# Attention and routed experts on one core: gathered tiles normalised by ScalarE, and no memsets between GpSimd's indirect transfers

## The reference

```
x = x + tanh(g_xattn) * attention(layernorm(x), ctx, ctx, Wq, bq, Wk, bk, Wv, bv)
n = layernorm(x)                         # (n - mean) / sqrt(var + 1e-5)
route = sigmoid(n @ Wr + br)             # 8 experts
e     = argmax(route);  p = max(route)
x = x + tanh(g_ffn) * p * (gelu(n @ W1[e]) @ W2[e])   # 128 -> 512 -> 128
```

## Time and profile before

| | |
|---|---|
| median of 3 runs | 146.72 us (146.46 to 148.03) |
| span of the profiled execution | 148.6 us |
| PE busy | 132.3 us, 89% |
| VectorE (DVE) busy | 96.4 us, 65% |
| ScalarE (ACT) busy | 77.9 us, 52% |
| GpSimd (POOL) busy | 121.3 us, 82% |
| DMA moved | 15.20 MB |

### The profile page before, as it was taken

How to read it: one execution, slowest core, us unless ns; L and a number is a source line. 1 busy time by engine, 2 the same in 40 slices (tenths; PEclk the granted TensorE clock), 3 DMA queues, 4 the chain that set the end, 5 groups by cost and what they waited for, 6 DMA issues and landing times.

```text
span 148.6 us, 4195 instructions
## 1 busy us (share of the span) xinstructions
PE 132.3 (89%) x1211; PEld 112.8 (76%) x1211; DVE 96.4 (65%) x532; ACT 77.9 (52%) x174; POOL 121.3 (82%) x198
## 2 busy tenths in 40 slices
PE   6989999989988976976899999999999999899690
PEld 2748777756755733854899899999999999899680
DVE  1698999997479999988659644455454345453230
ACT  0548597594584387328055274654555555454210
POOL 6538985887968988898998998998998998997354
PEclk9999999999999999999689999999999999999997
DMA  3999999911101151115413454551111100111000
GB/s 107 237 281 265 368 350 293 278 52 39 41 18 36 41 121 45 36 38 131 111 36 96 115 125 117 140 144 53 41 36 55 35 27 34 39 36 53 16 5 0
DMA packets 20080, 15.20 MB, mean 102 GB/s; under 512 B 6606, under 2 KB 16978, under 8 KB 20058
## 3 DMA queue, kind: packets, MB, share of 16 engines
q1 hardware_dynamic: 17328, 10.59, 27.2%
q0 software_dynamic: 2272, 4.27, 8.5%
q10 hardware_dynamic: 458, 0.08, 0.3%
HBM read 10.12 MB, written 5.26 MB: 103 GB/s over the span
## 4 chain that ended last, share of the span: by engine, by line
PE 53%; DVE 8%; issue 5%; POOL 1%; ACT 0%; DVEq 0%; POOLq 0%
PE banks_o L1309 24%; PE banks_v L1300 13%; PE bank_q L1300 5%; PE bank_p L1300 5%; PE bank_x L1292 3%; DVE rows L708 2%; PE bank_x L1172 1%; DVE stats L721 1%; POOL out_dram L448 1%; DVE tokn L926 1%; DVE rows L724 0%; DVE rows L775 0%; ACT hT L556 0%; DVE rank_max L742 0%; DVE tok L937 0%
## 5 line engine op out<-in xcount | busy, mean ns | idle before, releaser
L1309 PE MATMUL banks_o<-w_sb,hT 128*128 x312 | 42.6, 281 | 3.3 <-issue 1.8
L1309 PEld LDWEIGHTS banks_o<-w_sb,hT 128*128 128x128 f32 x312 | 38.5, 194 | 4.5 <-issue 4.4
L425 POOL DMA_INDIRECT scratch<-rows,row_at x32 | 31.8, 994 | 8.6 <-issue 4.5
L937 DVE SCALAR_TENSOR_TENSOR tok<-banks_o,tok 128x128 f32<-128x128 f32 x39 | 13.7, 350 | 35.3 <-PE banks_o L1309 22.5
L499 ACT COPY w_now<-w_sb 128x512 f32 x39 | 23.6, 611 | 10.3 <-issue 10.3
L442 POOL MEMSET unused<- 128x400 f32 x53 | 24.4, 461 | 0.0
L448 POOL DMA_INDIRECT out_dram<-tok x21 | 20.8, 991 | 3.5 <-issue 3.3
L448 POOL DMA_INDIRECT out_dram<-tok,token_at x18 | 17.7, 984 | 6.8 <-DVE tok L937 4.0
L1300 PE MATMUL banks_v<-toknT,w_now 128*128 128x128 f32 x160 | 22.0, 282 | 0.0
L556 ACT ACTIVATE hT<-banks_v 128x512 f32<-128x512 f32 x20 | 11.9, 596 | 17.5 <-PE banks_v L1300 10.7
L1300 PEld LDWEIGHTS banks_v<-toknT,w_now 128*128 128x128 f32 x160 | 20.3, 199 | 0.0
(11 more groups left out here) (176 smaller groups left out, 245.7 us busy)
## 6 DMA issues: line engine op xcount, KB each, us to landing
tok<-scratch SPq DMA_DIRECT2D x39, 66.0 KB, 2.2
x_all<-in_x_dram SPq DMA_DIRECT2D x8, 256.0 KB, 4.4
w_sb<-in_L_ffn_W_dram SPq DMA_DIRECT2D x1, 2048.0 KB, 10.5
ctx<-in_ctx_dram SPq DMA_DIRECT2D x8, 128.0 KB, 4.3
scratch<-pad_rows SPq DMA_DIRECT2D x1, 528.0 KB
scratch<-rows,row_at POOLq DMA_INDIRECT x32
out_dram<-tok POOLq DMA_INDIRECT x21
out_dram<-tok,token_at POOLq DMA_INDIRECT x18
```

The lines of the kernel that those rows point to most:

```text
L425: nc.gpsimd.indirect_dma_start(out=scratch, out_offset=bass.IndirectOffsetOnAxis(ap=row_at[:, g * GT + t:g * GT + t + 1], axis=0), in_=row ...
L937: nc.vector.scalar_tensor_tensor(out=tok[j][:, 0:D], in0=y_ps[j % 2], scalar=tok[j][:, SCALE:TOKEN], in1=tok[j][:, 0:D], op0=ALU.mult, op1 ...
L1309: last = nc.tensor.matmul(y_ps[j % 2], hT[j % DEEP][:, c * P:(c + 1) * P], w2_sb[:, bass.ds(w_at[j] + c * D, D)], start=(c == 0), stop=(c ...
```

## The change

The column of a row that held the mean now holds -mean * rstd, written by VectorE in a new instruction in `scale_logits`. `normalise_tile` moves from VectorE to ScalarE, as an Identity activation with that column as bias and rstd as scale. On ScalarE, `normalise_tile(0)` stands ahead of the first gelu, which loads the gelu table, `normalise_tile(1)` behind it, `normalise_tile(2)` behind the copies of W1 for tiles 2 and 3, and `normalise_tile(j + 3)` behind `gelu(j)` (and behind `tanh_logits` where there is one), ahead of `copy_w1(j + 4)`. `pause()` and its buffer and semaphore are gone, so that GpSimd's order keeps its transfers, its powers and its two normalisations alone.

```diff
-MEAN, RSTD, SCALE, TOKEN, ROW = 128, 129, 130, 131, 132
+SHIFT, RSTD, SCALE, TOKEN, ROW = 128, 129, 130, 131, 132
...
-            def pause():
-
-                if pauses[0]:
-                    pool.wait_ge(paused, pauses[0])
-                pauses[0] += 1
-                nc.gpsimd.memset(unused[:], 0.0).then_inc(paused, 1)
...
                 elif at in NORM_AT:
                     normalise_one(NG - 1, NORM_AT[at])
-                else:
-                    pause()
             for j in range(FFN_TILES):
                 scatter_tile(j)
-                if j < PAUSED:
-                    pause()
...
+            def normalise_tile(j):
+                if j < FFN_TILES:
+                    act.wait_ge(tok_in[j], 16)
+                    after(act, toknT_done, j - 2)
+                    nc.scalar.activation(tokn[j % 2][:], tok[j][:, 0:D], ACT.Identity, bias=tok[j][:, SHIFT:RSTD],
+                                         scale=tok[j][:, RSTD:SCALE]).then_inc(tokn_ready, 1)
...
+            normalise_tile(0)
             nc.scalar.activation(gelu_table[:], tanh_gates[:], ACT.Gelu)
+            normalise_tile(1)
             copy_w1(2)
             copy_w1(3)
+            normalise_tile(2)
             for j in range(FFN_TILES):
                 gelu(j)
                 if j == 1:
                     tanh_logits(NG - 2)
                 if j == 3:
                     tanh_logits(NG - 1)
+                normalise_tile(j + 3)
                 if j + DEEP < FFN_TILES:
                     copy_w1(j + DEEP)
...
                 nc.vector.tensor_tensor(scaled[:], rows[:, group(g), 0:E], column(g, RSTD).broadcast_to(wide), ALU.mult
                                         ).then_inc(scaled_done, 1)
+                nc.vector.scalar_tensor_tensor(out=column(g, SHIFT), in0=column(g, SHIFT), scalar=-1.0,
+                                               in1=column(g, RSTD), op0=ALU.mult, op1=ALU.mult)
...
-            def normalise_tile(j):
-                if j < FFN_TILES:
-                    dve.wait_ge(tok_in[j], 16)
-                    after(dve, toknT_done, j - 2)
-                    nc.vector.tensor_scalar(tokn[j % 2][:], tok[j][:, 0:D], tok[j][:, MEAN:RSTD], tok[j][:, RSTD:SCALE],
-                                            ALU.subtract, ALU.mult).then_inc(tokn_ready, 1)
```

More of the change, by code:

```diff
@@ L61, in attention_moe @@
     RSTD1_AT, NORM_AT = 2, {4: 0, 5: 1}
-    PAUSED = FFN_TILES - 8
     MOST = max(t1 - t0 for t0, t1 in STAGE_TILES)
@@ L149, in attention_moe @@
         place_of = sb("place_of", [P, GT, E])
-        unused = sb("unused", [P, 400])
         no_shift = sb("no_shift", [P, 1])
@@ L254, in attention_moe @@
         scattered = [sem(f"scattered{s}") for s in range(len(STAGES))]
-        paused = sem("paused")
         pads_ready, guards_written = sem("pads_ready"), sem("guards_written")
@@ L433, in _ @@
             normalise(6)
-            pauses = [0]
-            def pause():
-                if pauses[0]:
-                    pool.wait_ge(paused, pauses[0])
-                pauses[0] += 1
-                nc.gpsimd.memset(unused[:], 0.0).then_inc(paused, 1)
             def scatter_tile(j):
@@ L723, in bn_aggr2 @@
             def bn_aggr2(g, t):
-                return nc.vector.bn_aggr(rows[:, g * GT + t, E + MEAN:E + SCALE], stats2[:, t, :])
+                return nc.vector.bn_aggr(rows[:, g * GT + t, E + SHIFT:E + SCALE], stats2[:, t, :])
             def choose(c, step):
@@ L1069, in _ @@
                     take_tiles(0)
-            normalise_tile(0)
             sums(NG - 1)
@@ L1076, in _ @@
             residual(NG - 1, 1)
-            normalise_tile(1)
             choose(NG - 3, 0)
@@ L1084, in _ @@
             choose(NG - 3, 3)
-            normalise_tile(2)
             choose(NG - 3, 4)
@@ L1096, in _ @@
             aggregate2(NG - 1, 1)
-            normalise_tile(3)
             aggregate2(NG - 1, 2)
@@ L1108, in _ @@
             sum_tiles(1)
-            normalise_tile(4)
             pass_experts(1)
@@ L1122, in _ @@
                     choose(NG - 1, 1)
-                    normalise_tile(5)
                     choose(NG - 1, 2)
@@ L1127, in _ @@
                     copy_transposed(n + 1)
-                    if j > 0:
-                        normalise_tile(n + 2)
                 if j == 0:
```

## The result

The changed kernel took 143.67 us (median of 4 runs, 143.02 to 144.07) against 147.28 for the kernel before (4 runs, 146.46 to 148.03): a ratio of 0.974, 95% interval 0.969 to 0.979. That is faster, by 3.6 us where 2.9 were forecast. The same kernel was 9.5% slower on two chips it was run on later (ratios of 1.095 and 1.094), which no step of the prediction allows for. Both have to be explained.

The account below looks back on a forecast made before the run. PE bounds the stream of expert tiles, so only the start could gain: 3.0 us (1.6 clock, 1.3 order) less 0.1 for added VectorE work, memsets 0; 146.72 - 2.9 = 143.8 us, 8-in-10 range 143.0 to 146.8.

Parts of the forecast that it names:

- step 5: The start: with ScalarE normalising, PE transposes tile 5 at 68.05 instead of 69.81 and tile 7 3.0 us sooner.
- the bound of 70: Sign for the start: the prediction is wrong if `tanh(7)` on ScalarE lies beyond 70 us.
- the clock: Part of the start's gain: `down(2)` and `up(5)` on PE at 2.4 GHz instead of 1.2, 1.6 us.
- the order: Part of the start's gain: tile 5 no longer waits behind VectorE's routing of group 7, 1.3 us.
- rival B: ScalarE bounds the start, its queue behind tile 5's load making `tanh(7)` late: 148.1, up to 148.9 us; chance 0.10.
- steps 1 to 3: VectorE loses 39 `tokn`; ScalarE gains 39 at 515 ns, hidden in the stream; VectorE's eight added instructions cost 0.1 us.
- rival D: Identity under the gelu table forces ScalarE table loads, two per tile over 39 tiles: some 245 us; chance 0.02.
- step (4): GpSimd loses 53 memsets of 461 ns, 0.3 us won per transfer; counted as 0, bounds 0 and 0.4 us gained.
- 0.12 for slower: Chance given to the kernel being over 1% (1.47 us) slower.
- the prediction's own signs: It is wrong if `tanh(7)` lies beyond 70, the low clock remains, or the stream's beat exceeds 1.89 us.
- with nothing further recorded around it: Claim about the profiled execution before: span 148.6 us, 1.9 above the median of three runs (146.72).

Follow-up runs that it names:

- e8: The changed kernel with the 22 memsets among the scatters into scratch put back, none among the output transfers, on chip 3: 158.33 us, ratio 1.054.
- r2_before: The kernel before, without an edit, profiled again on chip 3: 149.42 us, ratio 0.998.
- e3: The kernel before with more filler matmuls on PE around the transpose of tile 5 (seven ahead, four behind), on chip 2: 152.09 us, ratio 1.005.
- r1_changed: The changed kernel, without an edit, run on chip 3: 164.41 us, ratio 1.095 to the kernel before.
- e1: The kernel before with only the memset pauses taken out, VectorE still normalising, on chip 2: 168.59 us, ratio 1.112.
- e2: The changed kernel with all 53 memsets put back, ScalarE normalising, on chip 2: 150.73 us, ratio 0.995 to the kernel before.
- e10: The changed kernel with all memsets, tile 5 normalised right behind tanh of group 7, PE's register reads ahead of its fillers, chip 4: 150.09 us, ratio 0.9925.
- e4: The changed kernel without the four filler matmuls ahead of the transpose of tile 5, on chip 2: 165.03 us, ratio 1.090 to the kernel before.

## Why the prediction was right, and where it failed

**Right: the start (step 5).** Transpose of tile 5 forecast at 68.05, measured 67.63; `down(2)` 69.5 and 68.76; `copy_transposed(5)` 70.2 and 69.59; `up(5)` 70.5 and 70.14; transpose of tile 7 73.0 and 72.42 on the chain; `tanh(7)` 69.0 and 68.18, well inside the bound of 70. Each is 0.4 to 0.8 us early, and so is the first load of stage 1 (issued at 64.63, forecast at 65.3). The 2.9 us from tile 0 to tile 7 stand between traces of two chips, but on chip 3 alone the transpose of tile 7 is 3.0 us earlier in e8 than in r2_before, which is the forecast (3.0, less 0.1). The split fits too: e3 gives the clock 1.5 us on PE (1.6 forecast), and from `down(1)` to `down(4)` PE needs 10.90 us in r2_before and 8.15 in e8, 2.75 less, which leaves 1.2 for the order (1.3 forecast). One number in rival B is off: by its own step of 1.5 us from the landing of tile 5 to `tanh(7)`, tile 5 at 68.7 gives 70.2 and not 69.8; nothing hangs on it.

**Right: the costs on ScalarE and VectorE (steps 1 to 3).** `tokn` takes 483 ns against 515 taken, within 411 to 615. There is no second table load, so rival D falls. ScalarE is busy 8.0 of 10 us in the stream (8.4 forecast), and the beat stays at 1.89. The added VectorE instructions take 0.15 us each (157 ns taken).

**Right as a number, wrong as a model: step (4).** The step was "I take 0 for the memsets, bounds 0 and 0.4 gained through less blocking of VectorE". The pitch of 1.28 us came as forecast (68.62, 69.89). On chip 1 nothing contradicts the price: no wait of the changed kernel was held there, and the 0.7 us by which 3.6 exceeds 2.9, above the upper bound of 0.4, is less than the four runs of before are apart. On three other chips the memsets are not free work to be taken away but what keeps the other engines' waits from being held: without them 1.112, 1.095 and 1.094, with them 0.995. The missing term is 5 to 8 us on the chain of waits for each of two rows of eight or more transfers (6.90 and 5.27 in r1_changed, 7.38 and 8.14 in e1), and the idle PE's low clock behind them. The prediction had no rival for this. Rival B looked for the loss at `tokn(5)` on ScalarE, and that did not happen in any run.

**The sign differed by the chip, which the chances didn't hold.** That 143.67 lies so near 143.8 is in part luck, for the sum holds only where this term is 0. 0.12 for slower came from rival B and D alone. Two of three chips on which the change itself was timed were slower by more than 9%, far outside of 143.0 to 146.8, and by the prediction's own signs it fails there: in r1_changed `tanh(7)` is at 78.22, beyond 70, and the clock falls again. The evidence that could have been read beforehand is the wait of 2.15 us at 139.97, at the only place in before where output transfers stand back to back while tiles still run.

**Wrong: "with nothing further recorded around it".** A time has 1.8 us around its span, so the profiled execution of before took some 150.4. That moved no term of the sum, which was a difference within one span.

**What stays open.** What holds the waits is not shown, only when: while GpSimd issues indirect transfers 1.3 us apart, in most rows until shortly after the last, in e8 and once in r1_changed released before it. Nor is it shown what makes chip 1 free of it. It runs a row of eight transfers (62.23 to 72.1) and one of 22 (73.19 to 101.2), all 1.3 us apart, with VectorE's and ScalarE's waits released at once. No version with memsets was run beside the changed kernel there, and the trace of the kernel before seems to be of another chip, so how the 0.974 splits between the two halves of the change isn't known.

## What to carry to other kernels

A filler instruction on an engine off the critical path may be what spaces its DMA issues; before it is deleted, look in the trace for a place where it is already missing, and for waits there that the profile puts down to nobody. A change to the pace of GpSimd's indirect transfers is to be timed on several chips, for here one kernel was 2.6% faster on one and 9.5% slower on two. And a gain at the start has to be followed tile by tile to the end, against a trace from the same chip: e8 was 2.9 us ahead of r2_before at tile 5 and 9.0 behind at the last tile.

## What the runs showed of the hardware

- **Waits held under a row of indirect transfers.** With transfers 1.27 to 1.29 us apart, VectorE's and ScalarE's waits for PE were released 6.5 and 7.4 us after PE was done (r1_changed), mostly 0.2 to 1.6 us after GpSimd's row ended. With a 0.46 us memset between them (1.59 us apart) waits "<-remote" of 1 to 3.6 us remained on chips 2 and 4 (e2, e3, e10) and none on chip 3 (r2_before, up to its last eight transfers); with one of 0.11 us, waits of 7.46 and 9.48.
- **Chips differ.** The kernel before took 147.3, 152.1, 149.7 and 151.4 us on four chips; the changed one 143.7, 164.4 and 166.0 on three of them.
- **The clock after idle time.** PE was idle 0.86 us before `down(2)` in the changed kernel, and 0.49 and 1.10 us on either side of a transpose in e4, and both times that `down` took 1.15 us at a granted clock of 1.00 (2.4 GHz). In the kernel before the same two gaps were 0.74 and 1.12 us, the granted clock was 0.50 behind them, and `down(2)` took 1.68. After 5.30 us of idle time in r1_changed `up(5)` took 1.94 at 0.50.
